# Adding the residual to the down projection of the first two chunks on TensorE, with ScalarE copying the bank out

## The reference, cut to what matters

```
mod = (silu(c) @ wmod).reshape(1, 6, 1, -1)       # sa, ca, ga, sb, cb, gb
h = layernorm(x) * (1 + ca) + sa
x = x + ga * ssm(h)       # h_t = exp(dt*A) * h_{t-1} + dt*B_t*x_t ; y_t = sum_n h_t[n]*C_t[n] + D*x_t
h = layernorm(x) * (1 + cb) + sb
g = (h @ gate_w.T) * gate_s
u = (h @ up_w.T) * up_s
x = x + gb * ((silu(g) * u) @ down_w.T * down_s)  # inner size 704
```

## Time and profile before

| | |
|---|---|
| runs of before | 315.71, 316.56, 316.79 us, median 316.56 |
| profiled execution | 314.61 us |
| its span | 312.8 us |
| busy in the span | TensorE 248.9, VectorE 256.8, GpSimd 227.0, ScalarE 183.7 us |
| mean granted TensorE clock | 0.874 of full speed |

### The profile page before, as it was taken

How to read it: one execution, slowest core, us unless ns; L and a number is a source line. 1 busy time by engine, 2 the same in 40 slices (tenths; PEclk the granted TensorE clock), 3 DMA queues, 4 the chain that set the end, 5 groups by cost and what they waited for, 6 DMA issues and landing times. The chain is left out here.

```text
span 312.8 us, 3793 instructions
## 1 busy us (share of the span) xinstructions
PE 248.9 (80%) x1226; PEld 185.5 (59%) x1226; DVE 256.8 (82%) x330; ACT 183.7 (59%) x294; POOL 227.0 (73%) x113
## 2 busy tenths in 40 slices
PE   7876799846387787848889997667899947897995
PEld 7634796435274455635658675446687835685874
DVE  3589966999999899969999999599988959944420
ACT  2688544765845976896349867932464883306400
POOL 1007789999999999979879997995599996700000
PEclk9995559997579889965999999958799995999999
DMA  7916897469262743392524735725636400001002
GB/s 249 327 48 162 156 143 203 69 104 233 73 133 72 137 103 107 72 147 28 124 69 108 161 90 118 135 38 151 167 90 149 118 1 0 2 0 67 2 0 71
DMA packets 33173, 33.09 MB, mean 106 GB/s; under 512 B 14912, under 2 KB 20224, under 8 KB 33152
## 3 DMA queue, kind: packets, MB, share of 16 engines
q1 hardware_dynamic: 32736, 32.01, 44.7%
q10 hardware_dynamic: 416, 0.81, 0.8%
HBM read 30.40 MB, written 2.36 MB: 105 GB/s over the span
## 5 line engine op out<-in xcount | busy, mean ns | idle before, releaser
L642 POOL TENSOR_TENSOR drv<-u,brow 128x1024 f32<-128x1024 f32 x63 | 147.8, 2362 | 21.0 <-DVE u L917 17.1
L830 ACT ACTIVATE decay<-delta,A 128x512 f32<-128x512 f32 x128 | 87.6, 688 | 82.9 <-DVE state L995 81.0
L995 DVE TENSOR_TENSOR_SCAN state<-decay,last,drv 128x512 f32<-128x512 f32 x96 | 119.1, 1268 | 11.7 <-ACT decay L830 11.4
L654 POOL TENSOR_TENSOR drv<-state,crow 128x1024 f32<-128x1024 f32 x29 | 68.7, 2369 | 9.9 <-DVE state L995 9.9
L1320 PE MATMUL sums<-ident,drv 128*128 128x128 f32 x512 | 72.1, 294 | 0.7 <-POOL drv L654 0.5
L1320 PEld LDWEIGHTS sums<-ident,drv 128*128 128x128 f32 x512 | 62.6, 151 | 12.0 <-issue 7.8
L969 DVE TENSOR_TENSOR drv<-state,rows_ps 128x1024 f32<-128x1024 f32 x35 | 41.8, 1195 | 5.4 <-PE rows_ps L1294 5.4
L1241 PE MATMUL side<-h_hi,ffn_hi 128*128 128x512 f32 x76 | 30.0, 479 | 18.6 <-DVE gates L942 16.1
L995 DVE TENSOR_TENSOR_SCAN state<-decay,drv 128x512 f32<-128x512 f32 x32 | 37.5, 1207 | 1.7 <-issue 1.1
L1294 PE MATMUL rows_ps<-c_parts,sel 64*128 64x512 f32 x35 | 19.6, 561 | 22.9 <-DVE drv L969 22.9
L1273 PE MATMUL side<-down_sb,gates 128*128 128x256 f32 x120 | 30.4, 403 | 4.3 <-DVE gates L953 3.5
(11 more groups left out here) (142 smaller groups left out, 291.9 us busy)
## 6 DMA issues: line engine op xcount, KB each, us to landing
brow<-bc_dram SPq DMA_DIRECT2D x31, 512.0 KB, 5.5
crow<-bc_dram SPq DMA_DIRECT2D x13, 512.0 KB, 7.0
resid<-in_x SPq DMA_DIRECT2D x4, 512.0 KB, 5.4
out<-resid SPq DMA_DIRECT2D x8, 256.0 KB, 2.2
gates<-in_wmod ACTq DMA_DIRECT2D x1, 768.0 KB, 6.1
gates<-in_wmod SPq DMA_DIRECT2D x1, 768.0 KB, 8.7
last<-state SPq DMA_DIRECT2D x48, 1.0 KB, 2.5
crow<-bc_dram SPq DMA_DIRECT2D x3, 256.0 KB, 3.7
```

Of the source, the lines that this page charges most:

```text
L642: nc.gpsimd.tensor_tensor(drv[j % RING_DRV][:, :, 0:S], u[:, c % 2, :, 0:S], b.unsqueeze(1).to_broadcast([P, HALVES, S]), ALU.mult).then_i ...
L654: nc.gpsimd.tensor_tensor(drv[j % RING_DRV][:, :, 0:S], state[j % RING_STATE][:, :, 0:S], row.unsqueeze(1).to_broadcast([P, HALVES, S]), A ...
L830: nc.scalar.activation(decay[i % RING_DECAY][:, 0:S], delta[:, c % 2, h, 0:S], ACT.Exp, scale=A[:, h * N + n:h * N + n + 1]).then_inc(deca ...
L995: nc.vector.tensor_tensor_scan(state[j % RING_STATE][:, h, 0:S], decay[i % RING_DECAY][:, 0:S], drv[j % RING_DRV][:, h, 0:S], before, ALU. ...
```

## The change

The task `out` moves from VectorE's lists to ScalarE's for chunks 0 and 1, half a slot to one slot later. In each down block of these chunks TensorE has one more fp32 product after the six: the identity matrix as weights and the block of `resid` (128 x 256) as data, accumulated into the same bank. ScalarE's `out` waits for the bank, copies 128x512 elements to `resid` and frees the bank. Chunks 2 and 3 keep VectorE's addition (L960).

```diff
 LATER = {
     "vector": [
-        (19, "K out0"), (22, "K out1"),
     ],
     "gpsimd": [],
-    "scalar": [],
+    "scalar": [
+        (20, "K out0"), (23, "K out1"),
+    ],
 SPREAD = {
     "vector": [
-        (21.5, "K out0"), (24.5, "K out1"),
     ],
     "gpsimd": [],
-    "scalar": [],
+    "scalar": [
+        (22, "K out0"), (25, "K out1"),
+    ],
...
+                elif name[:3] == "out":
+
+                    q = int(name[3:])
+                    src, i, k = side_bank(("K down", c, q))
+                    act.wait_ge(side_full[i], k + 1)
+                    b = BLK0[c] + 2 * q
+                    nc.scalar.activation(resid[:, b:b + 2, :].rearrange("p b d -> p (b d)"), src[:, :], ACT.Copy)\
+                      .then_inc(side_free[i], 1)
...
                     ins = nc.tensor.matmul(to, gates[REST:P, FULL, rows], down_sb[REST:P, FULL, :],
-                                           start=False, stop=True)
+                                           start=False, stop=c >= NCH - 2)
+                    if c < NCH - 2:
+
+                        ins = nc.tensor.matmul(to, ident[:, :], resid[:, BLK0[c] + b, :], start=False, stop=True)
                     if b % 2:
                         ins.then_inc(side_full[i], 1)
```

More of the change, by code:

```diff
@@ L110 @@
 LATER = {
-    "vector": [
-        (19, "K out0"), (22, "K out1"),
-    ],
-    "gpsimd": [],
-    "scalar": [],
+    "vector": [],
+    "gpsimd": [],
+    "scalar": [
+        (20, "K out0"), (23, "K out1"),
+    ],
     "tensor": [
```

## The result

The changed kernel takes 320.01 us (median of 4 runs, 319.17 to 320.96) against 316.68 (315.71 to 317.09): ratio 1.0113, 95% interval 1.0081 to 1.0145. That is +3.3 us where +2.46 was forecast (319.0), slower as forecast and inside the range.

What follows compares the result with a forecast made beforehand. The prediction took TensorE's full queue, feeding VectorE, as the bound where the change sits. Chunk 0's +1.07 and chunk 1's +1.39 sum to +2.46 us, median 316.56 to 319.0 us; range 316.5 to 320.4.

Steps and rivals of the forecast that it cites:

- What bounds: VectorE busiest on average, but fed by TensorE with little to spare; TensorE and ScalarE full where VectorE sheds 4.6 us.
- Chunk 0, +1.07: Step 2: three products delay row 8 of chunk 2 by 1.42 us, less slack 0.35, so VectorE waits 1.07 us.
- the 0.47: TensorE's time in us for one added fp32 identity product, two instructions of 0.236; bounds 0.24 and 0.63.
- ScalarE's part: Chunk 0: copies of about 0.6 us make decays of slots 6 to 8 0.57 late, hidden beneath row 8's delay.
- Chunk 1, +1.39: Step 3: four products delay gate4 by 1.89 us, less slack 0.50; Silu task and slot 11's scan 1.39 us late.
- the slack of 0.50: Chunk 1: gate4 ready at 246.22, its ScalarE copy at 246.72, so 0.50 us of TensorE delay is free.
- The sum: Whole kernel: 1.07 + 1.39 = +2.46 us, that is 7 x 0.47 - 0.85; median from 316.56 to 319.0 us.
- A: Rival: VectorE's time counts and its 4.6 us come back, 312.0 us, or half, 314.3 us; chance 0.09 for both.
- B: Rival: the identity product is cheap, one instruction or half the pitch; +0.8, 317.4 us; chance 0.10.
- C: Rival: TensorE's clock stays high at chunk 1's down blocks, gate4 isn't late; about +0.8, 317.4 us; chance 0.09.
- D: Rival: dearer, 0.63 us per product, one at low clock, or a late store or decay; +3.6 to +4, 320.4 us; 0.12.
- the second decay of slot 4 and the wait at out0 of chunk 1: Chunk 1: ScalarE waits at out0 for TensorE until about 228.7, copies, and that decay is ready at 231.0.

Runs made afterwards that it cites:

- e2: Changed kernel without the identity products: ScalarE copies the bank out and the residual is missing in the first two chunks; 315.98 us, ratio 1.0002.
- e5: Kernel before, with VectorE's four additions of the first two chunks cut to one column per block; ratio 0.9972.
- e9: Changed kernel with ScalarE's four copies cut to one column, all eight products and the bank wait kept; 320.46 us, ratio 1.0143.
- e6: Changed kernel with each identity product over 128 of the 256 columns; ratio 1.0084.
- e4: The change applied to chunk 1 alone, the other chunk as in the kernel before; 318.21 us, ratio 1.0063.
- e8: Changed kernel with TensorE's down3 one slot later in both chunks and ScalarE's out1 of chunk 0 half a slot later; 318.56 us, ratio 1.0052.
- e1: Changed kernel with the additions kept on VectorE while TensorE has the identity products; 324.48 us, ratio 1.0230.
- e3: The change applied to chunk 0 alone, the other chunk as in the kernel before; 319.27 us, ratio 1.0100.

## Why the prediction was right

**What bounds.** Right, by e2, e5 and e9: TensorE's queue feeds the scans here, and VectorE's 4.6 us are worth 0.85 at most.

**Chunk 0, +1.07.** Measured +1.12, with VectorE idle 1.16 us for row 8, as foretold (over 0.7). The three products lengthened the full stretch before row 8 by 1.44 us (22.08 to 23.52), 0.48 each, so the 0.47 was well sized, and 1.44 - 0.35 = 1.09. The 0.54 from a product's start to the next start is not what it adds: what stands behind it is 0.06 to 0.11 us shorter than behind the 64-row product (the eight instructions between down3 and row 8 take 0.97 us instead of 1.03, ten instructions of a down block 2.25 instead of 2.36). The sign "products at 0.47 us" was thus the wrong thing to look at. In e6 the same stretch grew by 0.81, 0.27 for each half product. ScalarE's part was hidden, as the text had it: e9 cuts the copies to 0.17 us and chunk 0 stays the same.

**Chunk 1, +1.39.** Measured +1.70 in the change and +1.86 in e4. The prediction's path is right, and closely: gate4's last matmul ends 2.17 us later in the change (from mark 2), 2.33 in e4, 1.55 in e6 and 2.29 in e8; less the slack of 0.50 that is 1.67, 1.83, 1.05 and 1.79, where 1.70, 1.86, 1.06 and 1.80 were measured. The term that was too small is the delay, taken as 1.89, and what it lacked is not a longer product but row 3 of chunk 3, which stands behind down1. Before, it ran beside down1's 64-row product (timeline of TensorE, before):

```profile
227.00 0.48 PE L1274 MATMUL side<-down_sb,gates 64*128 64x256 f32 x1
227.00 0.50 PE L1294 MATMUL rows_ps<-c_parts,sel 64*128 64x512 f32 x1
227.31 0.38 PE L1274 MATMUL side<-down_sb,gates 64*128 64x256 f32 x1
```

After, the identity product with its 128 rows stands between the two:

```profile
229.97 0.70 PE L1282 MATMUL side<-down_sb,gates 64*128 64x256 f32 x2
230.60 0.70 PE L1286 MATMUL side<-resid,ident 128*128 128x256 f32 x2
231.22 0.49 PE L1305 MATMUL rows_ps<-c_parts,sel 64*128 64x512 f32 x1
```

The row cost nothing before, since what follows the two begins at 227.62, as long after the 64-row product as without a row. After, what follows the row begins 0.42 us behind it. All six profiles without products in chunk 1 have the two starts within 0.01 us, all seven with them have the row alone. The kernel has the two in different halves of the partitions (REST is 64); that this lets them run together is likely, but no run tries it. Against the 0.42 stands down0 at another place of the clock, 4.64 before and 4.43 in the change. So 4 x 0.48 + 0.42 - 0.21 = 2.13, measured 2.17; for e4 4 x 0.48 + 0.42 - 0.05 = 2.29, measured 2.33; for e6 4 x 0.27 + 0.42 = 1.50, measured 1.55. That gate4 and not row 6 decides is shown by e8. The slack of 0.50 shows in e5 and e2 (-0.54 and -0.55, 0.05 of it the clock).

**The sum.** By the delays measured in the profile it is 1.44 + 2.17 - 0.85 = +2.8, and the two parts are +2.8; the prediction had +2.46. The runs say +3.3 by the medians, with an interval of the ratio from 2.6 to 4.6. The 0.5 between is within that interval. A candidate for it is the clock: a long low stretch costs 3.2 us and came in three of the thirteen profiles, all with the products; but the one profile of the change doesn't show it, so this stays open.

**Rivals.** A fell, with its cap as described: e2 and e5 got 0.7 and 0.85, not 4.6. B fell: two instructions. The page's figure for a matmul (the Trainium skill, "VectorE: DVE Perf Modes", section on the TRN2 errata) gives an estimate of 0.11 us per instruction of 256 columns; the trace has two instructions per fp32 product, which together add 0.48 us, so the measurement decides against it for this data type. C had the right place, and for the change itself the clock did little: low for 3.4 us in both, 0.2 us to its favour. I priced the case in which it stays high there and gave 0.4 us to a longer low stretch, when e1 and e9 show that it may last 10.2 us and cost over 3. D's size (0.63 for each product) wasn't reached. Of the signs to watch for, the second decay of slot 4 and the wait at out0 of chunk 1 came as described (1.08 us on ScalarE).

## What to carry to other kernels

Before moving work off the busiest engine, read the receiving engines in just that stretch: a queue that is full there, and that feeds the busy engine in order, turns each added instruction into delay, less only the slack of the next thing it feeds. Find that slack for each stretch as a difference of two rows (when it is ready, when it is used), and count what is put in front of it. Price an instruction by how much a full stretch grows, not by the distance to the next start: here 0.48 and not 0.54 us. Look also at what stood next to each other before: a product put between two instructions that ran together costs their overlap too, 0.42 us here. And mark a few instructions in both profiles and compare the parts between them: the whole span differed by 4.6 us, of which the change made 2.8.

## What the runs showed of the hardware that was not expected

An fp32 product of 256 columns with 128 rows, behind one with 64 rows, had 0.54 us to the next start, but three of them made a full stretch of TensorE 1.44 us longer, 0.48 each; with 128 columns it was 0.33 to the next start and 0.27 each in the stretch (e6). A row product of 64 rows and 512 columns began together with a 64-row fp32 product (227.00, before) and cost nothing; with a 128-row product between them it cost 0.42 us (all seven profiles with products in chunk 1). The granted clock is at its lower level for 3.4 us at the down blocks of chunk 1 in ten profiles and for 10.2 us in three, among them both of one kernel, at a cost of over 3 us; the product takes 1.01 us then. Even with 3.4 us in each, where it falls moved chunk 1's part by up to 0.2 us (e3, e4). Up to mark 1, in work that is the same in all kernels, thirteen profiles spread over 2.4 us.
